# Residual norm of a decoder: who normalises the last group, and in which order groups and tiles are transposed

## The reference

```python
def _layernorm(x, axis=-1, eps=1e-05):
    m = jnp.mean(x, axis=axis, keepdims=True)
    v = jnp.var(x, axis=axis, keepdims=True)
    return (x - m) / jnp.sqrt(v + eps)
...
x = _layernorm(x + _L0_attn_ref(x, ...), axis=-1)
x = _layernorm(x + _L0_xattn_ref(..., x, ctx_2048), axis=-1)
x = _layernorm(x + _L0_ffn_ref(x, ...), axis=-1)
...
```

## Time and profile before

| | |
|---|---|
| median of 3 runs | 5676.6 us (5672.98 to 5679.29) |
| the profiled execution | 5685.61 us |
| its span, first to last instruction | 5683.6 us |
| PE, DVE, ACT, POOL busy | 88%, 55%, 36%, 14% |
| mean granted clock of PE | 0.904 of full speed |

### The profile page before, as it was taken

One profiled execution on the slowest core, in us unless ns is written; L12 is line 12 of the kernel. 1 busy time (PEld: TensorE's weight loads), 2 busy tenths in 40 slices (PEclk: granted clock), 3 DMA queues, 4 the chain that ended last, 5 costly groups with the idle time before them and its releaser, 6 DMA issues. The chain is left out here.

```text
span 5683.6 us, 84525 instructions
## 1 busy us (share of the span) xinstructions
PE 5015.5 (88%) x33760; PEld 3280.5 (58%) x33760; DVE 3148.6 (55%) x5626; ACT 2020.8 (36%) x2774; POOL 803.4 (14%) x1216
## 2 busy tenths in 40 slices
PE   8349997799999999998788999982999998899898
PEld 5125554466666666665556777772555554555554
DVE  7862223778888888854305666555322225666322
ACT  3221112556665666542324554542111111333211
POOL 3000000243434343430200000000000001100000
PEclk7559998799999999998598999995999997799899
DMA  2114442122222222211000000000344441000133
GB/s 60 27 33 125 122 124 73 48 53 56 53 55 53 54 54 53 51 40 35 21 0 25 11 16 11 9 1 31 110 124 122 125 126 30 28 28 24 47 120 108
DMA packets 384766, 325.00 MB, mean 57 GB/s; under 512 B 238500, under 2 KB 279594, under 8 KB 383328
## 3 DMA queue, kind: packets, MB, share of 16 engines
q1 hardware_dynamic: 384384, 319.67, 19.9%
HBM read 284.57 MB, written 30.63 MB: 55 GB/s over the span
## 5 line engine op out<-in xcount | busy, mean ns | idle before, releaser
L558 DVE TENSOR_TENSOR f_act_g<-f_act_g,f_pu 128x512 f32<-128x512 f32 x288 | 198.1, 688 | 1092.8 <-ACT f_act_g L526 1092.8
L526 ACT ACTIVATE f_act_g<-f_pg 128x512 f32<-128x512 f32 x288 | 171.8, 597 | 1368.1 <-PE f_pu L480 1368.1
L2683 DVE SCALAR_TENSOR_TENSOR g_y<-a_f,a_cw,g_y 128x504 f32<-128x504 f32 x714 | 490.1, 728 | 207.1 <-ACT g_y L2544 201.9
L497 PE MATMUL f_py<-f_w_out,f_hidden 128*128 128x256 f32 x2304 | 550.9, 382 | 7.1 <-DVE f_hidden L563 7.1
L497 PEld LDWEIGHTS f_py<-f_w_out,f_hidden 128*128 128x128 f32 x2304 | 439.8, 191 | 195.2 <-issue 140.0
L480 PE MATMUL f_pg<-g_xT,f_w_in 128*128 128x512 f32 x1152 | 549.6, 600 | 0.0
L480 PE MATMUL f_pu<-g_xT,f_w_in 128*128 128x512 f32 x1152 | 543.7, 594 | 0.0
L2846 PE MATMUL a_f<-g_xT,a_w 128*128 128x512 f32 x952 | 449.7, 617 | 20.3 <-DVE g_y L2683 14.7
L480 PEld LDWEIGHTS f_pu<-g_xT,f_w_in 128*128 128x128 f32 x1152 | 220.4, 191 | 278.5 <-issue 278.5
L2846 PEld LDWEIGHTS a_f<-g_xT,a_w 128*128 128x128 f32 x952 | 181.6, 196 | 233.1 <-issue 223.3
L480 PEld LDWEIGHTS f_pg<-g_xT,f_w_in 128*128 128x128 f32 x1152 | 220.6, 192 | 163.2 <-issue 148.7
(11 more groups left out here) (487 smaller groups left out, 9007.3 us busy)
## 6 DMA issues: line engine op xcount, KB each, us to landing
f_w_in<-in_f_in_w SPq DMA_DIRECT2D x288, 256.0 KB, 2.9
f_w_out<-in_f_out_w SPq DMA_DIRECT2D x288, 128.0 KB, 2.0
f_scale<-f_comb SPq DMA_DIRECT2D x280, 128.0 KB, 3.2
f_scale<-f_comb SPq DMA_DIRECT2D x76, 256.0 KB, 3.4
a_c_row<-c_rows SPq DMA_DIRECT2D x128, 128.0 KB, 3.1
a_w<-in_a_w SPq DMA_DIRECT2D x16, 512.0 KB, 3.8
n_blocks<-a_N SPq DMA_DIRECT2D x256, 32.0 KB, 1.6
a_Nd<-n_blocks SPq DMA_DIRECT2D x64, 128.0 KB, 2.3
```

The source lines that it names most:

```text
L497: last = pe.matmul(py[b % 2][:, t, :], hidden[u][:, t * P:(t + 1) * P], w_out[v][:, :], start=False, stop=False, skip_group_check=True)
L558: dve.tensor_tensor(act_g[u][:, :], act_g[u][:, :], pu[u][:, :], ALU.mult).then_inc(gated, 1)
L2683: last = dve.scalar_tensor_tensor(out, v3(front(n, j)[:, :], SEQ)[:, :, 0:SEQ - back_by], cw[(n // NBLK) % 2][:, j, TAPS - 1 - back_by:TAP ...
```

## The change

The last group, 3, is normalised by DVE (four `tensor_scalar`, a new function `normalise_last`) right after the last scales and ahead of DVE's copies; ACT normalises groups 0, 1 and 2 only. PE transposes a tile at a time, both chunks of it, and waits before each tile for that tile alone; the groups come in the order 0, 1, 3, 2, and the copies and the last stage's stores follow the same order. ACT signals each tile instead of each group. Two semaphores are added, `last_normed` and `last_turned`.

```diff
--- before.py
+++ after.py
@@ -170,8 +170,9 @@
         mean2, gap, var, std, rstd, shift = (st.sb(m, [P, TILES]) for m in ("mean2", "gap", "var", "std", "rstd", "shift"))
         eps = st.sb("eps", [P, 1])
         pT = [st.ps(f"pT{g}", [P, KC, BLK]) for g in range(NBLK)]
-        dve_step, var_ready, std_ready, scaled, normed, turned, stored = (
-            st.sem(m) for m in ("step", "var_ready", "std_ready", "scaled", "normed", "turned", "stored"))
+        dve_step, var_ready, std_ready, scaled, normed, last_normed, turned, last_turned, stored = (
+            st.sem(m) for m in ("step", "var_ready", "std_ready", "scaled", "normed", "last_normed", "turned", "last_turned", "stored"))
+        LAST = NBLK - 1
         of = lambda g: slice(g * W, (g + 1) * W)
         with nc.Block() as block:
             @block.vector
@@ -198,8 +199,17 @@
                     dve.scalar_tensor_tensor(shift[:, of(g)], mean2[:, of(g)], -0.5, rstd[:, of(g)], ALU.mult, ALU.mult
                                              ).then_inc(scaled, 1)
 
+                def normalise_last():
+                    dve.wait_ge(scaled, NBLK)
+                    for t in range(LAST * W, TILES):
+                        dve.tensor_scalar(G.x_tok[:, t, :], G.x_tok[:, t, :], rstd[:, t:t + 1], shift[:, t:t + 1],
+                                          ALU.mult, ALU.add).then_inc(last_normed, 1)
+
                 def keep(g):
-                    dve.wait_ge(turned, g + 1)
+                    if g == LAST:
+                        dve.wait_ge(last_turned, 1)
+                    else:
+                        dve.wait_ge(turned, g + 1)
                     dve.tensor_copy(G.xT[:, 1, g * BLK:(g + 1) * BLK], pT[g][:, 1, :]).then_inc(stored, 1)
 
                 step(dve.memset(eps[:, :], LN_EPS))
@@ -211,8 +221,9 @@
                 spread(3)
                 scales(2)
                 scales(3)
+                normalise_last()
                 if out is None:
-                    for g in range(NBLK):
+                    for g in (0, 1, LAST, 2):
                         keep(g)
 
             @block.scalar
@@ -224,40 +235,54 @@
                 def normalise(g):
                     act.wait_ge(scaled, g + 1)
                     for t in range(g * W, (g + 1) * W):
-                        last = act.activation(G.x_tok[:, t, :], G.x_tok[:, t, :], ACT.Identity,
-                                              bias=shift[:, t:t + 1], scale=rstd[:, t:t + 1])
-                    last.then_inc(normed, 1)
+                        act.activation(G.x_tok[:, t, :], G.x_tok[:, t, :], ACT.Identity,
+                                       bias=shift[:, t:t + 1], scale=rstd[:, t:t + 1]).then_inc(normed, 1)
 
                 def keep(g):
-                    act.wait_ge(turned, g + 1)
+                    if g == LAST:
+                        act.wait_ge(last_turned, 1)
+                    else:
+                        act.wait_ge(turned, g + 1)
                     act.copy(G.xT[:, 0, g * BLK:(g + 1) * BLK], pT[g][:, 0, :]).then_inc(stored, 1)
 
                 root(0)
                 root(1)
-                for g in range(NBLK):
+                for g in range(LAST):
                     normalise(g)
                     if g + 2 < NBLK:
                         root(g + 2)
                     if out is None and g:
                         keep(g - 1)
                 if out is None:
-                    keep(NBLK - 1)
+                    keep(LAST)
+                    keep(2)
 
             if out is None:
                 @block.tensor
                 def _(pe):
-                    for g in range(NBLK):
-                        pe.wait_ge(normed, g + 1)
-                        for c in range(KC):
-                            for t in range(W):
+                    def turn(g, signal):
+                        for t in range(W):
+                            if g == LAST:
+                                pe.wait_ge(last_normed, t + 1)
+                            else:
+                                pe.wait_ge(normed, g * W + t + 1)
+                            for c in range(KC):
                                 last = pe.transpose(pT[g][:, c, t * P:(t + 1) * P], G.x_tok[:, g * W + t, c * P:(c + 1) * P],
                                                     G.ident[:, :])
-                        last.then_inc(turned, 1)
+                        last.then_inc(signal, 1)
+
+                    turn(0, turned)
+                    turn(1, turned)
+                    turn(LAST, last_turned)
+                    turn(2, turned)
             else:
                 @block.sync
                 def _(sp):
-                    for g in range(NBLK):
-                        sp.wait_ge(normed, g + 1)
+                    for g in (0, 1, LAST, 2):
+                        if g == LAST:
+                            sp.wait_ge(last_normed, W)
+                        else:
+                            sp.wait_ge(normed, (g + 1) * W)
                         sp.dma_start(out[:, of(g), :], G.x_tok[:, of(g), :]).then_inc(stored, 16)
                     sp.wait_ge(stored, NBLK * 16)
 
```

## The result

| | before | changed |
|---|---|---|
| median | 5672.98 us (7 runs, 5659.83 to 5684.38) | 5650.74 us (7 runs, 5641.48 to 5656.70) |
| ratio | | 0.9959, 95% interval 0.9946 to 0.9971 |
| profiled execution, span | 5685.6, 5683.6 us | 5648.6, 5646.5 us |
| granted clock of PE, mean | 0.904 | 0.912 |

Run again on another chip, the changed kernel gave 0.9956 (0.9943 to 0.9970). The forecast was 0.9950, inside both intervals. The forecast off the median was 5648 us with a range of 5638 to 5661.

What follows compares the result with a forecast made beforehand. Bound in a norm: ACT's normalising, then a whole group of transposes, then a copy. Norms 29.4 + last norm 1.9 - clears 1.5 - waits 1.1 = 28.7 us: 5656.9 profiled, 5648 off the median, range 5638 to 5661.

Steps and rivals of the forecast that it cites:

- The chain in a norm: First-form norm, start to last copy: 14.66 us at half clock or 13.54 at full, instead of 16.96.
- the norms that add y: Three norms that first add y: end at 19.71 us at half clock or 18.59 at full, instead of 22.00.
- Turning group 0 and 1 tile by tile brings nothing by itself: PE's first two groups in a norm: no gain, since ACT copies group 0 only behind normalising group 1.
- The share of norms at full clock: PE's sixteen transposes: full clock in a third of eleven norms, gaining 3.42 us each instead of 2.30.
- the waits' 1.1 us: PE's waits inside the sixteen transposes: 0.015 us each, seven per norm in eleven norms, a cost of 1.1 us.
- The last norm: Twelfth norm, which only stores: last store issued at about 5678.05 instead of 5679.91, a gain of 1.86 us.
- the landing behind it stays: End of the last norm: the time from the last store's issue to its landing was taken as unchanged.
- The clears: Behind each norm SP clears two more semaphores at 0.064 us each, 24 in all, a cost of 1.5 us.
- Sum: Whole kernel: 29.4 + 1.9 - 1.5 - 1.1 = 28.7 us gained, 0.50%.
- Pairs that don't overlap: Rival: each wait closes PE's pipe, 0.64 us per pair, norm ends at 16.07, whole gains 10.2 us; chance 0.11.
- Full clock everywhere: Rival: back-to-back transposes keep PE at full clock in all eleven norms, 38 us gained, 5639 by the median; chance 0.11.
- Slower stages: Rival: stages behind norms get full clock later, 80 us more at half clock, whole at 5690; chance 0.04.

Runs made afterwards that it cites:

- tile_only: Kernel before plus only ACT signalling each tile and PE transposing tile by tile; 5659.1 us, 0.9984 of the kernel before.
- group_turn: Changed kernel with PE waiting for whole groups again, DVE's share and order kept; 5652.4 us, 0.9967 of the kernel before.
- order_0123: Changed kernel with groups in the order 0, 1, 2, 3 on PE, in copies and stores; 5656.4 us, 0.9977 of the kernel before.
- more_sems: Changed kernel with 40 more unused semaphores per norm, cleared by SP; 5677.6 us, 1.0003 of the kernel before.
- warm: Changed kernel with PE doing zero matmuls (six or nine) at the start of each norm; 5635.4 us, 0.9932 of the kernel before.
- spread_clears: Changed kernel with semaphores cleared by all five engines, a fifth each, instead of SP alone; 5634.4 us, 0.9925 of the kernel before.
- waits_between: Changed kernel with DVE waiting for its own operation behind each of its four tiles; 5650.8 us, 0.9963 of the kernel before.
- warm_spread: Changed kernel with both zero matmuls at each norm's start and clears spread over five engines; 5630.7 us, 0.9922 of the kernel before.
- warm_mid: warm_spread plus zero matmuls between groups in the three norms that add y; 5631.6 us, 0.9934 of the kernel before.

## Why the prediction was right, and where it was not

- **The chain in a norm.** Right, step by step: DVE's four tiles 1.38 us against 1.37 worked out; PE's stretch at 10.23 against 10.22; the end 14.63 against 14.66 at half clock and 13.53 against 13.54 at full; the norms that add y 19.67 against 19.71. tile_only, group_turn and order_0123 were worked out in the same way and came out within 0.1 us.
- **"Turning group 0 and 1 tile by tile brings nothing by itself".** No run changes these two groups alone, but the norms come out as worked out without any gain from them. The prediction did not say what tile by tile brings in the last groups: 1.3 us of the 2.3 even without DVE's help (tile_only), 0.9 on top of it (group_turn).
- **The share of norms at full clock.** Taken as a third, worth 4.1 us. Two norms were fully so and three partly, and a1, which had the fast clock at its end before, gained only 2.04. Less the waits' 1.1 us the forecast was 28.3; measured is 28.2. This is partly luck, two misses of opposite sign: the full clock brought 2.9 us instead of 4.1, and the waits cost nothing: sixteen transposes with seven waits inside take 3.68 us, where 15 x 0.221 + 0.42 makes 3.73.
- **The last norm.** The step that failed is "the landing behind it stays": 0.8 us instead of 1.9. It was right for the issue, wrong for the transfer: with group 3 done on DVE the last two stores go out 0.4 us apart and share the DMA engines, in either order (order_0123), so the last lands 3.6 us after its issue instead of 2.6.
- **The clears.** 0.064 us each; 0.055 measured ((1.03 - 0.92) / 2), 0.057 to 0.069 in more_sems.
- **Sum.** 28.7 forecast, 27.8 found in the norms and gaps, 22 in the medians, with an interval of 16 to 31. The interval takes in both 27.8 and 28.7; the difference to the medians is not more than the stages scatter by. That the median of 5650.7 lies so near the forecast of 5648 is more than could be expected of a kernel whose stages moved by 9.3 us between the two profiles.
- **Rivals.** Pairs that don't overlap: excluded by the 3.68. Full clock everywhere: not in the changed kernel, but in two norms of it; warm shows that it can be had, and at what it was priced, 1.1 us per norm. Slower stages: between the two profiles single stages moved from 12.5 us shorter (a3) to 4.2 longer (f1), as the rival said they might; the sum over them was 9.3 us shorter, and by the medians some 6 us longer.

## What to carry to other kernels

Where a stage stands between two barriers, write down each engine's rows of one instance with the measured spacing, and move the work; the end of the stage comes out to a tenth of a microsecond, and the whole follows, though a kernel of this scatter shows it only to 7 us. Look at the engine behind the one that is relieved: without signalling tile by tile 0.9 of the 2.3 us would have been lost in front of PE. And when two transfers end a kernel, having both ready at once may only make them share the DMA engines; sending pieces as they become ready starts the transfer earlier.

## What the runs showed of the hardware

- A wait that is already met costs PE nothing measurable even at every second 128x128 transpose (sixteen in 3.68 us, 0.22 us apart at half clock).
- A semaphore clear costs SP 0.055 to 0.069 us on the path (more_sems); spread over five engines it is about 0.12 per clear of one engine, an estimate from spread_clears.
- On DVE four 128x256 operations with two per-partition scalars take 1.38 us without waits and 1.76 with one behind each (waits_between), at 407 and 413 ns of duration apiece; it is the spacing that changes.
- With six matmuls of zeros at the start of a norm PE's granted clock is 1.00 in the stretch of sixteen transposes, which begins 2.6 us behind them with groups 0 and 1 between, in 24 norms of 24 (warm, warm_spread, warm_mid); without them in 17 of 48.
- Two stores of 512 KB issued 0.4 us apart keep the 16 DMA engines 95% busy for 2.76 us, and the second lands 3.6 us after its issue; one alone takes 1.44 us at 90% and lands after 2.6.
